# Four stacked attention layers on one core: where one stage ends and the next begins

## The reference

```
x = x + tanh(g_xattn[l]) * attention_l(layernorm(x), ctx)   # l = 0..3
x = x + tanh(g_ffn[l])   * ffn_l(...)                       # l = 0..3
# layer 0: one head; feed-forward of 8 experts, top 2 (rows scattered to the experts' queues, results fetched back)
# layer 1: attention; feed-forward is the "searched network": six nodes with 8 heads each,
#          out = nodes[5];  layernorm(out, ln_g, ln_b)   with LN_EPS = 1e-6
# layer 2: attention with 16 heads of 16:
qh = q @ Wq.T + bq ; kh = k @ Wk.T + bk ; vh = v @ Wv.T + bv
attn = softmax(where(key_padding_mask, qh @ kh.T / 4, -inf))
return (attn @ vh) @ Wo.T + bo
# layer 2's feed-forward has ternary weights; layer 3: masked attention, then top 2 of routed experts
```

## Time and profile before

| what | value |
|---|---|
| runs | 3019.07 us median (3017.38 to 3025.81) |
| the profiled execution | 3024.15 us, its span 3022.4 us |
| mean granted clock of TensorE | 0.974 |
| busy: PE | 2883.5 us (95% of the span) |
| busy: DVE, ACT, POOL | 1934.6, 1313.8, 621.5 us (64, 43, 21%) |

### The profile page before, as it was taken

The page is one execution under the profiler, slowest core; times in us unless marked ns, Lnnn a source line. Parts: engine busy times, 40 slices in busy tenths (PEclk is TensorE's granted clock), DMA queues, the critical chain, the costliest instruction groups (busy, mean ns, idle before and its releaser), DMA issues. The chain is left out here.

```text
span 3022.4 us, 63586 instructions
## 1 busy us (share of the span) xinstructions
PE 2883.5 (95%) x24996; PEld 2189.2 (72%) x24996; DVE 1934.6 (64%) x3558; ACT 1313.8 (43%) x2493; POOL 621.5 (21%) x894
## 2 busy tenths in 40 slices
PE   7996999989999999999999999799999999899999
PEld 6873565667789999999999999666666666556444
DVE  5774111138677878788778877755656555589664
ACT  3431111126555555555555555445555555456000
POOL 3575000036300211023002400011111111036000
PEclk9997999999999999999999999999999999799999
DMA  9643223249500000000000000000000000346100
GB/s 286 216 137 101 95 105 110 78 145 273 163 1 1 2 2 1 2 1 2 2 2 2 2 1 1 1 27 24 24 19 24 24 24 19 107 126 214 51 14 21
DMA packets 80535, 185.11 MB, mean 61 GB/s; under 512 B 13541, under 2 KB 24306, under 8 KB 80020
## 3 DMA queue, kind: packets, MB, share of 16 engines
q1 hardware_dynamic: 63700, 140.99, 14.7%
q10 hardware_dynamic: 10208, 25.30, 2.8%
q0 software_dynamic: 6336, 14.76, 1.7%
HBM read 149.69 MB, written 27.84 MB: 59 GB/s over the span
## 5 line engine op out<-in xcount | busy, mean ns | idle before, releaser
L2818 DVE TENSOR_REDUCE top<-ps 112x2 f32<-112x750 f32 x256 | 228.6, 935 | 71.3 <-PE ps L3001 71.3
L1734 DVE TENSOR_TENSOR hidden<-gated,ps 128x512 f32<-128x512 f32 x64 | 44.0, 687 | 298.1 <-PE ps L1777 298.1
L2370 DVE TENSOR_REDUCE top<-ps 112x16 f32<-112x1792 f32 x96 | 194.2, 2023 | 46.2 <-PE ps L2609 46.0
L2912 ACT ACTIVATE probs_t<-ps 125x672 f32<-125x672 f32 x256 | 173.1, 728 | 71.6 <-PE ps L3029 71.6
L3495 PE MATMUL ps<-we,xn_t 128*128 128x512 f32 x448 | 201.4, 612 | 1.5 <-PEq L846 0.9
L2386 DVE TENSOR_TENSOR probs<-probs,inv_sum 112x1792 f32<-112x1792 f32 x96 | 195.9, 2041 | 3.3
L2374 DVE TENSOR_TENSOR probs<-ps,top 112x1792 f32<-112x1792 f32 x96 | 194.3, 2024 | 3.3
L2382 DVE TENSOR_REDUCE row_sum<-probs 112x16 f32<-112x1792 f32 x96 | 193.9, 2020 | 3.2 <-ACT probs L2494 3.2
L2577 PE MATMUL ps<-ident,probs 112*112 112x112 f32 x1536 | 179.8, 260 | 8.2 <-ACT probs_t L2489 7.3
L2489 ACT ACTIVATE probs_t<-ps 112x896 f32<-112x896 f32 x192 | 176.1, 917 | 15.2 <-PE ps L2577 3.7
L2568 PE MATMUL ps<-wv,nodes 128*112 128x256 f32 x768 | 181.4, 379 | 0.0
(11 more groups left out here) (476 smaller groups left out, 6021.3 us busy)
## 6 DMA issues: line engine op xcount, KB each, us to landing
ctx_t<-in_ctx_T_dram SPq DMA_DIRECT2D x96, 375.0 KB, 4.7
ctx_sb<-in_ctx_dram ACTq DMA_DIRECT2D x64, 384.0 KB, 4.2
ctx_sb<-in_ctx_dram SPq DMA_DIRECT2D x32, 384.0 KB, 7.3
ctx_sb<-in_ctx_T_dram SPq DMA_DIRECT2D x32, 375.0 KB, 3.1
queue<-zeros SPq DMA_DIRECT2D x32, 256.0 KB, 5.0
rows<-queue SPq DMA_DIRECT2D x16, 512.0 KB, 5.0
outputs<-out SPq DMA_DIRECT2D x16, 512.0 KB, 2.9
k_t<-pad_rows SPq DMA_DIRECT2D x512, 1.5 KB
```

The lines of the kernel that those rows point to most:

```text
L2370: dve.tensor_reduce(top[:, :, :], scores, AX.X, ALU.max).then_inc(s["top_done"], 1)
L2818: dve.tensor_reduce(tops[:, 2 * i:2 * i + 2], k.ps[0:S, at:at + 2, 0:L], AX.X, ALU.min).then_inc(s["tops_found"], 1)
```

## The change

Three things change.

*Exits.* A new `stage(nc)` only gives SBUF space back. It takes the place of `cleanup_on_exit` in six stages: mixture of experts, gathered attention, searched network, many-headed attention, masked attention, routed layer. Their semaphores are cleared by the next outer exit. `finish` goes, and its wait stands at the end of the routed layer's SP list.

*Landing waits.* POOL no longer waits for the last scatters in first attention; SP waits for them at the head of `run_experts`. SP no longer waits for the stores at the end of `run_experts`; POOL waits for the last two (the others are waited for in the order of their ring) ahead of its first fetch in gathered attention.

*Work across the border of the searched network and many-headed attention.* The searched network also computes the head constants (`key_constants`, 12 operations on DVE behind item 93), the statistics and norms of batches 0 and 1 (`first_statistics` behind item 94 on DVE, `first_norms`, 6 operations, at step 95 on POOL), and `gbo` (PE's two matmul instructions in step 97, into the scores' bank, and `gated_bias` on DVE). It finishes only group 12. Group 15 is copied to `xn` rather than `fin`. Many-headed attention finishes groups 13, 14 and 15 (`late_finish`), takes the statistics of 15, and starts with normed rows already there.

```diff
+@contextmanager
+def stage(nc):
+    base, top = nc.sbuf_base, nc.sbuf_top
+    yield
+    nc.sbuf_base, nc.sbuf_top = base, top
...
-def finish(k):
-    with k.nc.Block() as block:
-        @block.sync
-        def _(sp):
-            sp.wait_ge(k.stored, 16 * (TILES_R // 2))
...
 # masked, gathered, mixture, searched, many-headed, routed
-    with nc.cleanup_on_exit():
+    with stage(nc):
...
 # shared_scatters, POOL
-            if n % 4 == 3:
+            if n % 4 == 3 and (g < LAST or n + 1 < G * TOP_K):
                 pool.wait_ge(t.scattered[g], 16 * (n + 1))
-    for g in range(LAST + 1):
-        pool.wait_ge(t.scattered[g], 16 * G * TOP_K)
...
 # run_experts, SP
+                for scattered in t.scattered:
+                    sp.wait_ge(scattered, 16 * G * TOP_K)
...
-                for u in range(N):
-                    sp.wait_ge(rows_out[u], 16)
...
 # gathered_attention, POOL
                 def fetch(j):
+                    if j == 0:
+                        for rows_out in w.last_rows_out:
+                            pool.wait_ge(rows_out, 16)
...
 # searched_network, POOL
+                def first_norms():
+                    for j in range(2):
+                        pool.wait_ge(m.s["first_means"], j + 1)
...
+                pool.tensor_copy(m.gamma, w.gamma[:, :]).then_inc(m.s["gamma_kept"], 1)
...
+                    if t == ITEMS - 1:
+                        first_norms()
+                    if t in final_at and final_at[t] < GROUPS - 1:
                         scale_final(final_at[t])
...
 # searched_network, DVE
+                def gated_bias():
+                    dve.wait_ge(m.s["gbo_done"], 1)
+                    dve.tensor_tensor(m.gbo, k.ps[0:S, SCORE, 0:D], m.gbo, ALU.add).then_inc(m.s["gbo_added"], 1)
...
-                        if final_at[t] > TAIL:
-                            finish_tail(final_at[t] - 1)
+                        if final_at[t] == TAIL + 1:
+                            finish_tail(TAIL)
...
+                    if t == ITEMS - 3:
+                        key_constants()
+                    if t == ITEMS - 2:
+                        first_statistics()
+                    if t == ITEMS + 1:
+                        gated_bias()
...
 # searched_network, ACT: group 15 to xn
-                    if g >= TAIL + 2:
-                        act.wait_ge(s["fin_tailed"], 2 * PAIR * (g - 1 - TAIL))
+                    if g == TAIL + 2:
+                        act.wait_ge(s["fin_tailed"], 2 * PAIR)
+                    if g == GROUPS - 1:
+                        act.wait_ge(s["input_transposed"], GROUPS)
...
 # searched_network, PE
+                    if t == ITEMS + 1:
...
+                        pe.wait_ge(s["diff_done"], ITEMS)
+                        for c in range(DC):
+                            mm = pe.matmul(k.ps[0:S, SCORE, 0:D], m.bv_wide[:, c, :], m.wo_t[:, c, :], start=c == 0, stop=c == DC - 1)
+                        mm.then_inc(m.s["gbo_done"], 1)
...
 # many_headed_attention, DVE
+                def late_finish(i):
+                    first, fin, mean, rstd_ = w.late[i]
+                    if i == len(w.late) - 1:
+                        dve.wait_ge(w.s["late_rstd"], 1)
+                    for b in range(PAIR):
+                        dve.scalar_tensor_tensor(fin[:, b, :], fin[:, b, :], mean[:, b, 0:1], w.gamma, ALU.subtract, ALU.mult).then_inc(w.s["late_tailed"], 1)
...
+                late_finish(0)
+                late_statistics()
                 dve.memset(top[:, :, :], 0.0).then_inc(s["top_wiped"], 1)
...
+                    if n == FIRST + UNITS + 1:
+                        late_finish(1)
+                        late_finish(2)
...
 # many_headed_attention, PE
-                        pe.wait_ge(s["v01_copied"] if j else s["gbo_added"], max(j, 1))
+                        if j:
+                            pe.wait_ge(s["v01_copied"], j)
...
 # routed_layer, SP
+                sp.wait_ge(k.stored, 16 * (TILES_R // 2))
```

More of the change, by code:

```diff
@@ L2 @@
 from concourse import mybir
+from contextlib import contextmanager
 from itertools import count as counter
@@ L1641, in run_experts @@
         rows_in = [sem(nc, f"rows{u}_in") for u in range(N)]
-        rows_out = [sem(nc, f"rows{u}_out") for u in range(N)]
+        rows_out = [sem(nc, f"rows{u}_out") for u in range(N - 2)] + w.last_rows_out
         names = "transposed rows_copied gate_done gated_done up_done hidden_done down_done out_copied"
@@ L2160, in early_edge, with mixture_of_experts @@
     return home[:, q % 2 * DC * D:(q % 2 + 1) * DC * D].rearrange("p (c d) -> p c d", c=DC)
-def mixture_of_experts(k, w, net):
+def mixture_of_experts(k, w, t, net):
     nc = k.nc
-    with nc.cleanup_on_exit():
+    with stage(nc):
         for _ in range(1, EXPERT_RING):
             expert_slot(k, w)
-        run_experts(k, w, net)
+        w.last_rows_out = [sem(nc, f"last_rows{u}_out") for u in range(2)]
+        run_experts(k, w, t, net)
 H2, HD2 = 16, D // 16
@@ L2650, in _ @@
                         attend(t - 2)
+        m.late = [(PAIR * g, fin[:, g % 2, :, :] if g < GROUPS - 1 else xn[:, :, :], fin_mean_var[:, g % 2, :, :], fin_rstd[:, g % 2, :]) for g in range(TAIL + 1, GROUPS)]
+        m.late_stats, m.late_var_eps = fin_stats[:, (GROUPS - 1) % 2, :, :], fin_var_eps[:, (GROUPS - 1) % 2, :]
 TERNARY_GROUPS = ((0, 2), (2, 6), (6, 11), (11, 13), (13, 16))
@@ L3120, in project_v01 @@
                     mm.then_inc(s["v01_done"], 1)
-                pe.wait_ge(w.s["weights_loaded"], 64)
-                pe.wait_ge(w.s["bv_spread"], 1)
-                for c in range(DC):
-                    mm = pe.matmul(k.ps[0:S, SMALL, 0:D], w.bv_wide[:, c, :], w.wo_t[:, c, :], start=c == 0, stop=c == DC - 1)
-                mm.then_inc(s["gbo_done"], 1)
                 for n in range(FIRST, LAST):
```

134 lines of the change are left out of this document (82 added, 52 removed).

## The result

The changed kernel took 3002.26 us (median of 4 runs, 2999.16 to 3004.44), the kernel before 3021.6 beside it (3017.38 to 3025.81). The ratio is 0.9932, with a 95% interval of 0.9918 to 0.9946, that is 16 to 25 us less. A second series gave 3001.43 us and 0.9938 [0.9925, 0.9951]. The forecast was 3005 us, within 2997 to 3013.

A forecast was written before the change was run, and what follows sets the result against it. PE, busy 95% of the 3022.4 us span, bounds the kernel; time comes from its idle time and half-clock stretches. Terms -1.3 - 1.4 - 1.7 - 9.8 = -14.2 us, from the median 3019.07 to 3004.9, forecast 3005, range 2997 to 3013.

The forecast's parts named there:

- Stage exits: At six stage ends: an exit costs 0.46 us plus its clear; removal saves, less +0.5 clearing at the end: -1.3 us.
- First attention's end: POOL's drain, a fixed price of about 5.3 us, begins earlier without the wait for the last scatters: -1.4 us.
- Experts' end: Without SP's wait for stores, POOL's first fetch in gathered attention starts at 645.4 and not 647.12: -1.7 us.
- Rival 1: Experts' end: PE's shorter idle time keeps the clock up, 6.7 us gained in place of 1.7, so 3000 us; 8%.
- Searched to many-headed: Border of these stages: earlier barrier -4.3, one exit less -0.46, earlier first k product -5.07: sum -9.8 us.
- k product: Many-headed attention's start: PE's first k product should come 0.8 us after the last barrier, where it took 5.87.
- rival 2: Many-headed attention's head: DVE becomes the bound, 2.1 us return, that term is -7.7, the time 3007; 12%.
- The clock: PE's six half-clock stretches may each shift with the work ahead; direction unknown, 3 us on either side.
- Rival 4: Ternary stage: its dense part keeps the lower clock, making the kernel slower, 3029 us if half runs there; 4%.
- The drain's record: Sign at first attention's end: POOL's drain should be 5.3 us again; a longer one means rival 3.
- rival 3: First attention's and experts' ends: moved landing waits buy 0 for 1.4 and 0.3 for 1.7, so 3007.7 us; 12%.
- The last barrier: Sign: the last barrier before many-headed attention should fall at 1948 to 1951 us in the changed trace, from 1958.0.

The follow-up runs named there:

- exits_only: The kernel before with only the six stage exits and the last block taken out: 3017.53 us, ratio 0.9985 [0.997, 1.0].
- border_only: The changed kernel with exits and landing waits put back as before, leaving only the work moved across the searched/many-headed border: 3012.97 us, ratio 0.9977.
- waits_only: The kernel before with only the landing waits moved, and the experts' exit gone: 3021.38 us, ratio 1.0 [0.9986, 1.0014].
- exit_out: The kernel before with only many-headed attention's exit taken out: 3017.75 us, ratio 0.9993 [0.9982, 1.0004].
- mask_first: The changed kernel with the first q mask put ahead of group 13's finish and the late statistics on DVE: 3000.17 us, ratio 0.9935.
- pool_wipe: mask_first with the two wipes of v on GpSimd and not on DVE: 3002.08 us, ratio 0.9933 [0.9906, 0.996].

## Why the prediction was right, by its steps

*Stage exits* (-1.3). Right. By the rows of the pair it is -0.4 at gathered attention, -0.7 and -0.6 for the two exits that go whole, and +0.5 at the end, -1.2 in all. The clear at the end grew by 0.42 (0.5 forecast); the landing of the last store bounds the end as before, and the end comes 1.8 us after SP's leave where it came after 1.3. exits_only gives -4.5 us, with an interval of 0 to -9, and its profile has a ternary block by 7 us shorter; an exit's own price is seen better in 0.8 for one against 1.2 for two.

*First attention's end* (-1.4). Right, with -1.7 (8.1 to 6.4 in each of the seven profiles). The rule that the prediction takes from the Trainium skill (page "PSUM — Partial Sum Buffer", section "Engine vs sequencer instructions"), that a drain waits for the engine to go fully idle, agrees with its record of 8.6 us. But the part after the last issue is the same 5.3 as the drain had before, so the term is not 0.

*Experts' end* (-1.7). Right in place and about in size. The fetch gained 1.35 and the other engines 2.65. From the last store's issue to gathered attention's end it is 174.6 us on average over the seven profiles with the old waits and 172.4 over the seven without: -2.2, with 4.5 and 6.3 us of scatter inside the groups. In the first pair alone it is -1.0. The experts' block got another 0.6 us shorter ahead of that store (3.0 in all, of which 2.4 are the wait), which I had not forecast. It goes with the clock: the stretch at 0.50 around the start of that block is 23.9 us long in all seven profiles with the old waits and 20.5 in the seven without. Here it is in the kernel before and in the changed one:

```profile
277.00:300.80 23.80, 7.71 (x15) 0.50 0.54 162
272.10:292.50 20.40, 6.42 (x14) 0.50 0.55 163
```

Rival 1, that the clock would stay up there, did not come: it still fell, for 3.4 to 10.2 us in all seven without the old waits.

*Searched to many-headed* (-9.8). The place and the sum were right, two terms inside were not. From the last exit before the searched block to the many-headed block's end it is 1790.0 before and 1779.4 after, -10.6: in the searched block -3.9 with one exit less (-0.4), and -6.3 behind. Barrier and k product came where the steps put them (0.55 us after the barrier, 0.8 forecast). The cover on DVE held, but less than said: the mask came 1.77 us late for PE, not 0 to 0.4, because I had timed PE's queue at the lower clock, and full clock came back 3.4 us after the barrier: PE asked for the mask at 6.1 and not at 7.4 to 7.9. DVE's own queue was timed well (mask over at 7.8, as forecast). From the first k product to the first scores it took 11.0 us in place of 11.75 in spite of the 1.77, so the clock gave back about 2.5 us (an estimate, 0.7 + 1.77). So rival 2's place was right, and its price was paid out of a gain that the forecast did not have. That the two nearly cancel is luck. The clock's part is the same in every profile: at this border PE stood at 0.50 for 13.7 or 17.1 us in the six profiles without the moved work, and for 3.4 us in the seven changed ones (in border_only for 3.4 twice).

*The clock* (0, give or take 3). This is the term that was mis-sized. The prediction counted six stretches at the lower clock; the trace before has 18, the changed one 18 as well, but 158 us in all against 117. The ternary block took 62.4 to 62.8 us in the six undelayed profiles of the changed kernel and its variants, with and without the exit in it. It took 68.8, 68.6, 68.6 and 66.0 in the two of the kernel before, border_only and waits_only, and 61.8 and 61.9 in exits_only and exit_out. The mean of these other six is 65.9, so 3.4 us on average, 6.4 in the first pair; by what the runs of exit_out say, the 3.4 is a rough estimate. Rival 4 looked at this place with the other sign.

The timed runs say more than single profiles here, since each has its mean granted clock on record. In the 70 runs of the kernel before that were timed beside the experiments, the time goes with it: 0.978 at 3010.93 us, the shortest, and 0.971 at 3034.43, the longest. Worked out from clock and span, each us more at the lower clock goes with 0.44 us more of time (correlation 0.92). The kernel before has 0.975 on average, about 153 us at the lower clock. The changed kernel has 0.979, about 125. At 0.44 each, these 28 us would make 12 of the 19.3 (an estimate). Part of them is the border's and so in the -10.6 already, and a correlation does not tell cause from effect. But it says where to look for what the forecast lacked, and that the spread of the kernel before's runs is for the most part that of its clock.

Sum by these columns: -1.7, -3.0 and +0.1 (gathered, means 171.6 and 171.7), -0.4 for its exit, -10.6, -3.4, +1 for masked attention (the extra stretch of 3.4 us), -0.4 at the end: -18.4. The medians say -19.3. What stays open is what decides how long a stretch lasts, and why the changed kernel came to the short distance each time.

The total came closer than the terms did. The forecast of 3005 was counted from 3019.07 us; beside the changed kernel, the kernel before took 3021.6, from which the same terms give 3007.4. Of the signs named in advance, the k product came (0.55 us after the barrier). The drain's record was longer than 5.3 us, which was to mean rival 3, but its end, 5.3 us after the last issue, speaks against it: the sign was badly chosen. The last barrier came at 1944.6 and not at 1948 to 1951, for 5.4 us that lay ahead of the last scatter. The first fetch came 1.35 and not 1.7 us earlier, with 1.7 more of DVE's wait behind it, and the ternary stretches did not keep their lengths. PE waited for DVE at the mask, as rival 2 has it.

## What to carry to other kernels

Where PE is 95% busy, look at the barriers between stages: move the last groups' work that nobody waits for behind the barrier, and the next stage's constants before it, under the idle time of the engine that holds them. When the idle time shrinks, the clock may come back earlier (here 3.4 us after the barrier and not 12.0), so time the covers at full clock, or the next engine in line will seem to have spare time that it hasn't. A landing wait belongs to the one that reads what landed; here that is seen in the profiles, not in the runs. And look at the granted clock of every run, not only of the profiled one, before you explain a stage's length by an edit.

## What the runs showed of the hardware

- GpSimd's drain at a block's end took 5.29 us in first attention, and ended 5.3 us after the last indirect DMA's issue was over when no wait stood between.
- Equal work at the ternary stage's start met 17, 21, 24, 27 or 31 us of the lower clock. It was 17 in all nine profiles in which it began 7.0 to 8.4 us after the fall, and 24 to 31 in the three with 9.0 to 9.4; 10.4 gave 21, and 6.0 gave 27. What decides is not shown.
- PE's idle times of 2.55 us (changed kernel, at 1944.6) and 2.94 us (border_only, at 1950.4) came with a fall of the clock, as those of 5.03 and 8.51 us did before.
- While GpSimd added to x (two operations, 1.69 us from 1954.29 in mask_first), DVE's pair at 1954.45 took 1.81 us instead of 0.87, and GpSimd's own took 1.69 instead of 1.41. pool_wipe shows the same two numbers. In the changed kernel they do not meet. These 0.9 us are more than the 0.7 by which mask_first's scores came earlier, so this is probably where its gain went; no run took them apart.
